# Delta-rule stage: four 32-row products per slot written as one 128-row product over a block diagonal, twice a slot

## The reference, cut to what matters

```
def step(S, inp):
    qt, kt, vt, gt, bt = inp
    S = S * jnp.exp(gt)[..., None]
    vd = (vt - jnp.einsum('bhkv,bhk->bhv', S, kt)) * bt[..., None]
    S = S + kt[..., None] * vd[:, :, None, :]
    return (S, jnp.einsum('bhkv,bhk->bhv', S, qt))
```

## Time and profile before

| | |
|---|---|
| time, median of 3 runs | 3394.72 us (3394.36 to 3396.34) |
| the profiled execution's own time | 3396.07 us |
| its span, first to last instruction | 3394.3 us |
| mean granted TensorE clock | 0.976 |
| units 0 to 14 of the stage, K(0) of unit 0 to K(0) of unit 15 | 900.00 to 2676.98 us |
| unit 15 | 2676.98 to about 2763 us |

### The profile page before, as it was taken

One profiled execution on the slowest core, in us unless ns is written; L12 is line 12 of the kernel. 1 busy time (PEld: TensorE's weight loads), 2 busy tenths in 40 slices (PEclk: granted clock), 3 DMA queues, 4 the chain that ended last, 5 costly groups with the idle time before them and its releaser, 6 DMA issues. The chain is left out here.

```text
span 3394.3 us, 78389 instructions
## 1 busy us (share of the span) xinstructions
PE 3237.4 (95%) x33424; PEld 1532.6 (45%) x33424; DVE 2161.3 (64%) x3580; ACT 1488.2 (44%) x3420; POOL 125.9 (4%) x457
## 2 busy tenths in 40 slices
PE   8999999997889999999999999999999869999999
PEld 4444444443444444444444444444444434444443
DVE  2454425425789888888878888888898526451441
ACT  2221102204566765776676577567667533110110
POOL 0000000000000000000000000000000000000000
PEclk9999999998989999999999999999999779999999
DMA  3031322122101111121111211111211012222211
GB/s 121 0 90 60 88 78 65 47 74 88 40 30 42 36 61 37 33 76 46 39 52 44 66 33 52 43 40 42 67 43 36 12 70 91 66 87 76 61 56 68
DMA packets 97945, 191.53 MB, mean 56 GB/s; under 512 B 10184, under 2 KB 35400, under 8 KB 95296
## 3 DMA queue, kind: packets, MB, share of 16 engines
q1 hardware_dynamic: 97600, 186.51, 17.6%
HBM read 171.54 MB, written 14.94 MB: 55 GB/s over the span
## 5 line engine op out<-in xcount | busy, mean ns | idle before, releaser
L1734 PE MATMUL psum<-dl_xt,dl_wqkv 128*128 128x512 f32 x1536 | 761.7, 619 | 9.6 <-DVE dl_qkv L1373 9.6
L1373 DVE SCALAR_TENSOR_TENSOR dl_qkv<-psum,dl_par,dl_qkv 128x511 f32<-128x511 f32 (+2 forms) x576 | 428.9, 745 | 33.9 <-ACT dl_tails L1212 24.9
L521 PE MATMUL psum<-xnt_sb,wmats 128*128 128x512 f32 x896 | 408.9, 593 | 1.1 <-DVE f_partial L789 1.1
L1734 PEld LDWEIGHTS psum<-dl_xt,dl_wqkv 128*128 128x128 f32 x1536 | 262.4, 190 | 265.6 <-issue 229.8
L521 PE MATMUL psum<-f_token_sums,wmats 128*128 128x512 f32 x672 | 306.8, 592 | 0.0
L789 DVE TENSOR_TENSOR f_partial<-f_partial,psum 128x512 f32<-128x512 f32 x112 | 77.1, 688 | 311.2 <-PE psum L521 309.9
L521 PEld LDWEIGHTS psum<-xnt_sb,wmats 128*128 128x128 f32 x896 | 169.1, 190 | 214.1 <-issue 207.9
L1741 PE MATMUL psum<-dl_wo,dl_sg 128*128 128x512 f32 x512 | 256.7, 620 | 0.1
L672 ACT ACTIVATE f_partial<-psum 128x512 f32<-128x512 f32 x32 | 19.1, 597 | 510.5 <-PE psum L521 510.5
L1208 ACT ACTIVATE dl_qkv<-psum,dl_par 128x512 f32<-128x512 f32 x192 | 149.1, 776 | 197.8 <-PE psum L1734 197.8
L577 PE MATMUL psum<-f_wdown,f_hidden_b 128*128 128x512 f32 x512 | 221.7, 593 | 3.4 <-DVE x_sb L812 3.4
(11 more groups left out here) (232 smaller groups left out, 4738.0 us busy)
## 6 DMA issues: line engine op xcount, KB each, us to landing
dl_wqkv<-in_dw_qkv SPq DMA_DIRECT2D x192, 256.0 KB, 2.6
f_wdown<-in_wdowns SPq DMA_DIRECT2D x64, 512.0 KB, 3.6
wmats<-in_wmats SPq DMA_DIRECT2D x56, 512.0 KB, 3.5
dl_wo<-in_dwo SPq DMA_DIRECT2D x16, 1024.0 KB, 5.5
f_weights_b<-f_weights_by_expert SPq DMA_DIRECT2D x24, 512.0 KB, 9.1
x_sb<-in_x SPq DMA_DIRECT2D x4, 1024.0 KB, 9.1
x_after_experts<-x_sb SPq DMA_DIRECT2D x16, 256.0 KB, 2.6
dl_wfb<-in_dwfb SPq DMA_DIRECT2D x16, 256.0 KB, 3.4
```

The source lines that it names most:

```text
L521: ins = pe.matmul(ps[:, bank, :], wm[:, m % WRING, block, k, :], moving[:, k, :], start=(fresh and k == 0), stop=(last_of and k == 1), ski ...
L1373: tap_ = lambda dl: dve.scalar_tensor_tensor(y_[:, dl:TT], ps[:, bank, 0:TT - dl], par[:, h, 4 * a + 3 - dl:4 * a + 4 - dl], y_[:, dl:TT], ...
L1734: last = pe.matmul(ps[:, bank, :], wq[:, n % RING, m, :], xt[:, u // HG % 2, m, :], start=(m == 0), stop=(m == KC - 1))
```

## The change

`zd` is no longer scaled in place. Its four blocks of a chunk are scaled and written onto the diagonal of a 128 by 128 matrix, `zblocks[:, g]`, one DVE instruction for each head (32 partitions): for chunks 0 to 3 in `corner_in` (slot 0), for chunks 4 to 15 at the end of slot 2. `solve_u` is then one product of 128 rows and 128 columns. For `output_inner`, DVE writes the four blocks of `amat` onto a diagonal, `ablocks[:, sl % 2]`, in every slot, ahead of `add_state`; the product is one too. The off-diagonal parts are zeros. To make room: `zd` and `ga` have one buffer instead of two (the `ga` job moves from unit w's slot 7 to unit k's, one unit later), `beta`, `bnt` and the unit matrix `eye` lose theirs (`beta` lies in `half`, `bnt` in `small`, and y = 1 - nd is made by a negation and 16 additions on its diagonal), and ACT's scratch `junk` moves from SBUF to bank 3 of PSUM.

```diff
+        zblocks = sb("zblocks", [P, NG, P])
+        ablocks = sb("ablocks", [P, 2, HJ, C])
+        junk = ps[:, 3, mid]
...
+                pool.memset(zblocks[:], 0.0)
...
+                def a_blocks(k, sl):
+
+                    n = SLOTS * k + sl
+                    if n >= 2:
+                        dve.wait_ge(s["o_ps"], n - 1)
+                    heads = cst[:, K_JM:K_JM + HJ].unsqueeze(2).broadcast_to([P, HJ, C])
+                    dve.tensor_tensor(ablocks[:, sl % 2], amat(k)[:, sl, 1, :].unsqueeze(1).broadcast_to([P, HJ, C]), heads,
+                                      ALU.mult).then_inc(s["a_ready"], 1)
...
-                    dve.tensor_tensor(y, eye, nd, ALU.subtract).then_inc(s["blocks_ready"], 1)
+                    step(dve.tensor_scalar(y, nd, -1.0, None, ALU.mult))
+                    diagonal = y.rearrange("p t s -> p (t s)")[:, 0:HB * HB:HB + 1]
+                    dve.tensor_scalar(diagonal, diagonal, 1.0, None, ALU.add).then_inc(s["blocks_ready"], 1)
...
-                    dve.tensor_tensor(zd(u), zd(u), kb1.unsqueeze(2).broadcast_to([P, NG, C]),
-                                      ALU.mult).then_inc(s["z_ready"], 1)
+                    if u > 0:
+                        dve.wait_ge(s["u_ps"], SLOTS * u)
+                    z_blocks(u, 0)
+
+                def z_blocks(u, part_of):
+
+                    gs = (slice(0, 4), slice(4, NG))[part_of]
+                    for j in range(HJ):
+                        rows = part(j)
+                        last = dve.tensor_tensor(zblocks[rows, gs, C * j:C * j + C], zd(u)[rows, gs, :],
+                                                 kb1[rows, gs].unsqueeze(2).broadcast_to([C, gs.stop - gs.start, C]), ALU.mult)
+                        if j < HJ - 1:
+                            o.done(last)
+                    last.then_inc(s["z_ready"], 1)
...
                         if run:
+                            a_blocks(k, sl)
                             add_state(k, sl)
...
+                        if run and sl == 2:
+                            z_blocks(k, 1)
...
-                    for j in range(HJ):
-                        last = pe.matmul(ps[part(j), OPS, mid], amat(u)[part(j), g, 1, :], ubuf[part(j), g % 2, :],
-                                         start=False, stop=True, skip_group_check=True)
-                    last.then_inc(s["o_ps"], 1)
+                    pe.matmul(ps[:, OPS, mid], ablocks[:, g % 2].rearrange("p j t -> p (j t)"), ubuf[:, g % 2, :],
+                              start=False, stop=True, skip_group_check=True).then_inc(s["o_ps"], 1)
...
-                    for j in range(HJ):
-                        last = pe.matmul(ps[part(j), UPS, mid], zd(k)[part(j), sl, :], rbuf[part(j), :], start=True, stop=True)
-                    last.then_inc(s["u_ps"], 1)
+                    pe.matmul(ps[:, UPS, mid], zblocks[:, sl, :], rbuf[:, :], start=True, stop=True).then_inc(s["u_ps"], 1)
```

More of the change, by code:

```diff
@@ L46 @@
 RING = 3
[L49 to L52, removed]
+K_ID, K_ONE, K_JM, K_MASK, K_EPS5, K_EPS6, K_JLT = 0, 128, 129, 133, 325, 326, 327
+K_N = 391
+D_ROW, D_M0 = 0, 64
+D_N = 66
 def constants():
@@ L60, in constants @@
     c[:, K_ID:K_ID + P] = np.eye(P)
-    c[:, K_ONE:K_ONE + P] = 1.0
+    c[:, K_ONE] = 1.0
     c[p, K_JM + p // C] = 1.0
@@ L85, in delta_constants @@
     p = np.arange(P)
-    c[:, D_EYE:D_EYE + HB * HB] = np.eye(HB, dtype=np.float32).reshape(-1)
-    for m in range(8):
+    for m in range(2):
         c[:, D_ROW + m * C + m] = 1.0
@@ L947, in short_jobs @@
              (15, "inner"): [("vrow", w, 0, every), ("corner", w, 0, first)], (15, "end"): [("corner", w, 0, second)]}
-    once = {(4, "end"): ("beta", w, 0, every), (7, "end"): ("ga", w, 0, every), (9, "end"): ("fa", w2, 0, every)}.get((sl, at))
+    once = {(4, "end"): ("beta", w, 0, every), (7, "end"): ("ga", k, 0, every), (9, "end"): ("fa", w2, 0, every)}.get((sl, at))
     jobs = [once] if once and once[1] % HG == 0 else []
@@ L996, in delta_stage @@
         amat2 = sb("amat", [P, 2, NG, 2, C])
-        zd2 = sb("zd", [P, 2, NG, C])
+        zd1 = sb("zd", [P, NG, C])
+        zblocks = sb("zblocks", [P, NG, P])
         state = sb("state", [P, H, P])
@@ L1002, in delta_stage @@
         fa = sb("fa", [P, TT])
-        ga = sb("ga", [P, 2, TT])
+        ga = sb("ga", [P, TT])
         sg = sb("sg", [P, HJ, TT])
@@ L1020, in delta_stage @@
         ubuf = sb("ubuf", [P, 2, P])
-        junk = sb("junk", [P, P])
+        ablocks = sb("ablocks", [P, 2, HJ, C])
         KK, QQ, VV = 0, 1, 2
@@ L1025, in delta_stage @@
         m0, m1 = dcs[:, D_M0:D_M0 + 1], dcs[:, D_M0 + 1:D_M0 + 2]
-        eye = dcs[:, D_EYE:D_EYE + HB * HB].rearrange("p (t s) -> p t s", s=HB)
         one_row = dcs[:, D_ROW:D_ROW + 2 * C].rearrange("p (m c) -> p m c", c=C)
         nd, y, ytmp = half[:, 0], half[:, 1], half[:, 2]
+        beta = half[0:H, 0:2].rearrange("p n t s -> p (n t s)")
         bt, kb1, kbd, kbt, kbs = (small[:, n] for n in range(5))
         kb1 = kb1[:, 0:NG]
+        bnt = small[:, 3:5].rearrange("p n c -> p (n c)")[:, 0:9 * HJ].rearrange("p (a j n) -> p a j n", a=3, j=HJ)
         def cbuf(u, a):
@@ L1048, in delta_stage @@
         kq, kkt, val, amat, zd = (lambda u: kq2[:, u % 2]), (lambda u: kkt2[:, u % 2]), (lambda u: val2[:, u % 2]), (
-            lambda u: amat2[:, u % 2]), (lambda u: zd2[:, u % 2])
+            lambda u: amat2[:, u % 2]), (lambda u: zd1[:])
         kap, nkap, oss, tot = (lambda u: kap2[:, u % 2]), (lambda u: nkap2[:, u % 2]), (lambda u: oss2[:, u % 2]), (
@@ L1061, in delta_stage @@
         b_dram = nc.dram_tensor("betas", [H, TT], F32).ap()
-        names = """tails_ready const_ready par_in onw_in dc_in kps r_ready u_ps u_ready s_ps s_read sd_ready o_ps o_read o_squared tapped
+        names = """tails_ready const_ready par_in onw_in dc_in kps r_ready u_ps u_ready s_ps s_read sd_ready o_ps a_ready o_read o_squared tapped
             bnd_ready edged q_silu k_silu v_silu k_square q_square softplus_abs softplus_exp softplus_ln series_done softplus_sum decay_ready
@@ L1189, in take_o @@
                     act.wait_ge(s["o_read"], n + 1)
-                    act.activation(junk[:, :], val(u)[:, g, :], ACT.Square,
+                    act.activation(junk, val(u)[:, g, :], ACT.Square,
                                    accum_out=oss(u)[:, g:g + 1]).then_inc(s["o_squared"], 1)
@@ L1251, in short @@
                         if u > 0:
-                            act.wait_ge(s["beta_out"], 16 * (u // HG))
+                            act.wait_ge(s["halves"], u)
                         act.activation(beta[:, :], ps[0:H, bank, :], ACT.Sigmoid).then_inc(read[bank], 1)
                     elif kind == "ga":
-                        copy_out(ga[:, u // HG % 2, :], *job)
+                        if u > 0:
+                            wait_full(act, "gate", u - 1, 3)
+                        copy_out(ga[:, :], *job)
                     elif kind == "fa":
@@ L1801, in short_job @@
                             wait_read(pe, "ga", u - u % HG, 0)
-                        last = pe.matmul(ps[:, bank, :], wgb[:, P * n:P * n + P], ga[:, u // HG % 2, :], start=True, stop=True)
+                        last = pe.matmul(ps[:, bank, :], wgb[:, P * n:P * n + P], ga[:, :], start=True, stop=True)
                     elif kind == "dec":
```

7 lines of the change are left out of this document (3 added, 4 removed).

## The result

The changed kernel takes 3414.3 us (median of 5 runs, 3412.45 to 3417.61), the kernel before 3395.94 (5 runs): a ratio of 1.0056, interval 1.0046 to 1.0067, slower by 18.4 us. The forecast was 3408, from a sum that came to 3412.

What follows compares the result with a forecast made beforehand. PE was taken to bound slots 13-15 and 4, DVE nearly everywhere else. Profiled 3396.07 + 3 (work) + 14 (clock drops) = 3413, median 3412; stated as 3408 since drops may be rarer, range 3378 to 3426.

Steps and rivals of the forecast that it cites:

- main forecast: Whole kernel: DVE's additions cost some time and longer PE waits lower the clock; 3408 us, chance 0.45.
- PE's saving: `solve_u` and `output_inner` on PE: 6.2 us a unit, about 100 in all, were PE alone the limit.
- DVE's additions: New DVE instructions: 0.21 us per `ablocks`, 2.24 for late `zblocks` in slot 2, 0.55 in slot 0, 0.15 in slot 11.
- the rival in which they overlap: DVE's additions overlap like its other instructions, so slots 0-3 cost less: 3385 us without drops; chance 0.17.
- Unit 9: Slots 0-1 +0.67, 2-3 +0.47, 4-6 0.0, 7-12 +0.92, 13-15 -1.11: sum +0.95 us.
- the term of small waits of DVE that go: Slots 7-12 of unit 9: 0.14 us of small waits taken off DVE's additions, R(12) coming 1.06 later.
- All units: Six units of +0.95, eight of about -0.3, unit 0 +2.4, unit 15 -3: together +3 us.
- The moved `ga` job: Moves from one place in slot 7 to the same place a unit later: cost 0.
- The wait and the clock: PE's wait ahead of slot 12's `solve_u` grows to 2.5 us in about 13 units; ten drops of 1.4: +14.
- The 1.0 us at K(12) and U(11): Part of the grown 3.5 us wait falling at slot 12's `keys_state` and slot 11's `solve_u`: about 1.0 us.
- second rival: DVE's additions overlap like its other instructions: 3385 us without the drops, 3379 if `ablocks` takes 0.15; chance 0.17.
- the first: Rival for the whole kernel: the same without the clock falling, 3395 + 3 = 3398 us; chance 0.25.

Runs made afterwards that it cites:

- e1: Changed kernel plus four unread products of 256 columns on PE ahead of slot 12's `solve_u`, except in units 2, 4, 6, 10: 3405.54 us (1.0027).
- e2: Changed kernel with only `solve_u` as a single product; `output_inner` has four products again, no `ablocks`: 3394.86 us (0.9998).
- e3: Changed kernel with only `output_inner` as a single product; `zd` scaled in place, four products in `solve_u`: 3398.1 us (1.0008).
- e7: Changed kernel, GpSimd writing `ablocks` and `zblocks` of chunks 1 to 15, slot 12's transposes and decay product ahead of `solve_u`: 3373.17 us (0.9936).
- e4: Changed kernel with all `ablocks` and the `zblocks` of chunks 4 to 15 written by GpSimd instead of DVE: 3373.94 us (0.9933).

## Why the prediction was right

The cause and the size were those of the main forecast, the size in part by luck, since terms that were off cancelled; point by point:

- **PE's saving.** 0.14 us for `output_inner`: 0.35 and an exposed load before, 0.32 to the next start after, as worked out. Slots 13-15: -0.98, forecast -1.11.
- **DVE's additions.** The four late `zblocks` take 2.28 us from first start to last end, forecast 2.24: each starts about 0.03 after the end of the one before it. The trace agrees with the rule on held instructions that the prediction draws on (the Trainium skill, VectorE: DVE Perf Modes, Two Vector instructions with no wait between them), and the rival in which they overlap falls. `ablocks` do overlap, by the 0.08 us of the row used: each puts the next instruction off by 0.20, where 0.21 was said.
- **Unit 9.** +0.67, +0.54, -0.03, +0.57, -0.98 for +0.67, +0.47, 0.0, +0.92, -1.11. The sum is +0.77 for +0.95; the step most mis-sized is slots 7-12, where R(12) came 0.65 later and not 1.06. Five `ablocks` are 1.00 there for 1.05, the negation and additions about 0.1 for 0.15; what was sized too small is the term of small waits of DVE that go, 0.14 in the forecast and some 0.4 in the trace.
- **All units.** Less the drops units 0-14 are 5.8 us longer; the forecast's terms for them give 6 x 0.95 - 8 x 0.3 + 2.4 = 5.7. That they agree so well is luck: units 1 to 13 lost 1.9 for a forecast of 2.35, unit 0 1.3 for 2.4, and unit 14, with its longer stretch at the lower clock, 2.6 for 0.95. Unit 15 gained 1.1 to its last `state_step`, forecast 3. The stage also began 1.05 us sooner, which was no term. The moved `ga` job shortened units 3, 7 and 11 by 1.3 to 3.1 us and lengthened units 4, 8 and 12 by 4.2 to 5.1, drops included; that it comes to little in sum was right.
- **The wait and the clock.** Forecast 2.5 us ahead of U(12) in 13 units; measured 2.0 to 2.2 in ten of 15, 1.7 in three, 0.4 and 3.9 in the others (3.9 in the kernel before too). The 1.0 us at K(12) and U(11) was 0 to 0.4 at K(12) and none at U(11). Forecast ten drops of 1.4 us, measured eight of 1.6, one of them not behind U(12)'s wait: 14 and 12.8. The experiments show it as the cause: e1 takes six drops away with more work on PE, e2 and e3 have half the change each, a shorter wait, and no drop and two. What the prediction set against the Trainium skill's advice (TensorE: Matmul & The Clock Gate, Why this matters for your kernels), which speaks only of gaps over some 3 us, held: idle times of 1.7 ("issue", e7, unit 8) to 2.2 us were followed by the lower clock.
- **From 3412 to 3408.** The sum was +17 us. At the last `state_step` the profiled execution is 16.4 us behind the one before, at the stage's last instruction 17.2 and at the end 18.2; the last 1.0 arises in work that the change doesn't touch, and stays open. The drops were rarer, as allowed for, but each cost more; the 4 us taken off were too much.
- **A slip.** The second rival's 3385 is the first's 3398 less 10, so 3388; nothing else hangs on it.

What also stays open: why of ten equal waits ahead of U(12) seven are followed by a drop and three are not, and why of six waits of 2.0 in e4 and of seven of 1.8 to 2.0 in e3 only two each are.

## What to carry to other kernels

Before packing small matmuls into one, ask who prepares the packed operand: here some 6 us of VectorE time a unit (16 x 0.20, 2.28, 0.65 more for the early blocks, about 0.1) bought 6.2 us of TensorE time, by the prediction's sum, and for the most part where VectorE was the limit. The same packing with most of that work on GpSimd made the kernel 0.7% faster, and 1% with the two jobs moved, of which the move alone gives 0.2 to 0.3%. A faster engine ahead of an unchanged wait makes the wait longer, and the TensorE clock can fall behind it, here behind some idle times of 1.7 us and more, and cost more than was saved; move work that is due anyway into the wait. Work given to GpSimd belongs beside VectorE instructions that read PSUM, not beside TENSOR_SCALARs between SBUF tiles.

## What the runs showed of the hardware

- The halves don't add: -1 and +2 us apart, +18 together. Six more drops of the clock, behind one wait that each half lengthens, make 9.6 us of that.
- In units 1 to 13, waits of TensorE of 0.7 and 1.1 us ahead of U(12) were followed by no drop of the clock, seven of 1.84 to 2.03 in e3 and six of 2.0 in e4 by two drops each; of the changed kernel's ten of 2.0 to 2.2, unit 0's included, seven were. An idle time of 1.67 us was followed by one in e7, three of 1.66 to 1.69 in the changed kernel by none.
- GpSimd beside VectorE: medians of 403 ns for 128 x 128 float32 and 826 for 32 x 384 (1.4 and 1.5 times VectorE's), up to 2413 and 1697, and up to 0.6 us more for the VectorE instruction (1218 to 1473 and 1800 ns), without a semaphore between them.
- Four VectorE products that write to four quarters of the partitions do not overlap (2.28 us for four of 0.547), while one over all partitions beside neighbours like it puts the next off by 0.20 of its 0.28.
